# Attention ends, router and expert layer of a four-layer hybrid network rewritten, the shared expert's gate and up projections in one product

## The reference, cut to what matters

```python
t = t + _L2_attn_ref(_ln_t(t))
t = t + _L2_ffn_ref(_ln_t(t), ...)
t = t + _L3_attn_ref(_ln_t(t), ...)
t = t + _L3_ffn_ref(_ln_t(t), ...)

def _L3_ffn_ref(x, router, shared_gate, shared_up, shared_down, W_gate, W_up, W_down):
    # n = 2048 tokens, D = 128, E = 8 experts, TOP_K = 2, H = 64
    shared_out = silu(x @ shared_gate) * (x @ shared_up) @ shared_down
    probs = softmax(x @ router)
    topk_scores, topk_idx = top_k(probs, TOP_K)      # combine[n, e] = score, or 0
    gate = silu(einsum('nd,edh->enh', x, W_gate))
    up = einsum('nd,edh->enh', x, W_up)
    y = einsum('enh,ehd->end', gate * up, W_down)
    return shared_out + einsum('ne,end->nd', combine, y)
```

## Time and profile before

| | us |
|---|---|
| median of 3 runs | 683.55 |
| lowest and highest run | 678.59, 688.02 |
| profiled execution, its own time | 681.39 |
| its span, first to last instruction | 679.7 |
| PE, DVE, ACT, POOL busy | 587.7, 416.9, 339.5, 285.6 |

### The profile page before, as it was taken

One profiled execution on the slowest core, in us unless ns is written; L12 is line 12 of the kernel. 1 busy time (PEld: TensorE's weight loads), 2 busy tenths in 40 slices (PEclk: granted clock), 3 DMA queues, 4 the chain that ended last, 5 costly groups with the idle time before them and its releaser, 6 DMA issues. The chain is left out here.

```text
span 679.7 us, 10150 instructions
## 1 busy us (share of the span) xinstructions
PE 587.7 (86%) x3280; PEld 322.6 (47%) x3280; DVE 416.9 (61%) x858; ACT 339.5 (50%) x586; POOL 285.6 (42%) x656
## 2 busy tenths in 40 slices
PE   7897898894965999999999999995589998469997
PEld 6664455552755444444444444443346666443332
DVE  3553477761552877678997999797545654144343
ACT  3542356663343866766667757682314555132321
POOL 4564012334141777777868776791101223300000
PEclk9997899996785999999999999998799999569999
DMA  6800000000000000000000000000000000000000
GB/s 175 237 1 0 1 2 2 2 1 0 1 2 0 1 0 0 1 1 0 1 0 0 2 0 0 1 0 0 2 1 2 1 2 2 0 0 1 30 16 16
DMA packets 10246, 8.62 MB, mean 13 GB/s; under 512 B 4042, under 2 KB 8148, under 8 KB 10196
## 3 DMA queue, kind: packets, MB, share of 16 engines
q1 hardware_dynamic: 10196, 8.00, 4.1%
HBM read 6.94 MB, written 1.05 MB: 12 GB/s over the span
## 5 line engine op out<-in xcount | busy, mean ns | idle before, releaser
L1477 POOL TENSOR_TENSOR h_s<-g_s 128x512 f32<-128x512 f32 x128 | 163.9, 1284 | 53.3 <-ACT g_s L1411 34.2
L1411 ACT ACTIVATE g_s<-z_s,b 128x1024 f32<-128x1024 f32 x128 | 146.9, 1149 | 65.2 <-DVE z_s L1334 38.6
L1334 DVE TENSOR_TENSOR z_s<-bank,PB 128x1024 f32<-128x1024 f32 x128 | 153.5, 1219 | 31.8 <-PE bank L1269 31.4
L1269 PE MATMUL bank<-XN_C,W 128*128 128x512 f32 x256 | 130.2, 594 | 0.9 <-PEq L1069 0.9
L1276 PE MATMUL bank<-h_s,W 128*128 128x512 f32 x256 | 130.3, 593 | 0.1
L983 DVE TENSOR_REDUCE shiftpad<-bank 128x2 f32<-128x512 f32 (+1 forms) x128 | 72.3, 588 | 66.2 <-PE bank L812 35.8
L966 ACT ACTIVATE ET_all<-bank 128x512 f32<-128x512 f32 (+1 forms) x128 | 59.2, 514 | 75.9 <-PE bank L829 43.9
L1276 PEld LDWEIGHTS bank<-h_s,W 128*128 128x128 f32 x256 | 48.5, 190 | 62.0 <-issue 56.9
L1269 PEld LDWEIGHTS bank<-XN_C,W 128*128 128x128 f32 x256 | 47.0, 190 | 52.7 <-issue 44.6
L1036 POOL TENSOR_SCALAR var<-mv 128x2 f32<-128x2 f32 x16 | 3.5, 222 | 142.2 <-DVE mv L1023 142.1
L824 PE MATMUL bank<-Qp,Kp 17*128 17x256 f32 x256 | 36.4, 401 | 7.3 <-DVE Qp L996 7.2
(11 more groups left out here) (280 smaller groups left out, 1013.0 us busy)
## 6 DMA issues: line engine op xcount, KB each, us to landing
W<-in_L_ffn_W_dram SPq DMA_DIRECT2D x1, 2048.0 KB, 8.9
out_dram<-y_s SPq DMA_DIRECT2D x4, 256.0 KB, 2.2
XN_T<-in_x_dram SPq DMA_DIRECT2D x3, 256.0 KB, 5.1
XN_T<-in_x_dram SPq DMA_DIRECT2D x2, 128.0 KB, 2.2
Wgate<-in_L_ffn_W_gate_dram SPq DMA_DIRECT2D x1, 256.0 KB, 5.0
Wup<-in_L_ffn_W_up_dram SPq DMA_DIRECT2D x1, 256.0 KB, 4.3
Wdown<-in_L_ffn_W_down_dram SPq DMA_DIRECT2D x1, 256.0 KB, 4.0
wraw<-in_L_conv_W_qkv_dram SPq DMA_DIRECT2D x1, 192.0 KB
```

The lines of the kernel that those rows point to most:

```text
L1269: nc.tensor.matmul(bank[s % 4][:, :], W1[:, f // 4, f % 4 * P:(f % 4 + 1) * P], XN_C[:, g * W:(g + 1) * W], start=True, stop=True).then_in ...
L1334: nc.vector.tensor_tensor(z_s[:, s % RING, :].rearrange("p (w n) -> p w n", w=2), bank[s % 4][:, None, :].broadcast_to([P, 2, W]), PB[:, g ...
L1411: nc.scalar.activation(g_s[:, s % RING_G, :], z_s[:, s % RING, :], ACT.Gelu, bias=b1[:, f:f + 1]).then_inc(s_g, 1)
L1477: nc.gpsimd.tensor_tensor(h_s[:, s % RING, :], g_s[:, s % RING_G, 0:W], g_s[:, s % RING_G, W:2 * W], ALU.add).then_inc(s_h, 1)
```

## The change

- The attention blocks of layers 1 and 3 end when image 6 is in XN_C (step 41). Image 7's root, scaling, turning and storing move to the front of the next block (class `LastImage`): VectorE computes the root there in 12 linked steps, 11 of them linked to the next, instead of GpSimd's 16. In layer 2 this stands at VectorE's step 1, ScalarE's steps 2 and 3 and TensorE's step 3; in the expert block at the very start and at steps 0 and 1.
- In layer 2's attention the last pair's root is also computed by VectorE, not by GpSimd.
- The router block is gone. Its work is split into two halves of 8 tiles (class `ExpertWeights`, with 17 VectorE pieces numbered 0 to 16: 0 and 1 maximum and subtraction, 2 to 4 the softmax, 5 the MAX8, 6 the index search, 7 to 11 the mask, 12 to 16 the three bf16 parts). The early half runs inside layer 3's attention, its logits at steps 19, 23, 27 and 31, its VectorE pieces at steps 32 to 38, its turns and stores at steps 40 and 41. The late half runs inside the expert block's steps 2 to 9.
- The expert block is written out, 20 steps q with no loop, down products lag by two steps (before: one, inside a group), a_s and c_s have four buffers each, and two result banks take turns.
- The shared expert's gate and up weights lie side by side (Sboth), so one product gives gate on partitions 0 to 63 and up on 64 to 127. ScalarE reads rows 0 to 63 and writes its Silu to rows 64 to 127, where VectorE multiplies it with the up rows; the shared down product reads rows 64 to 127.
- The residual is no longer turned ahead and added by VectorE: four products of R with the identity per group open the result bank's accumulation. VectorE copies the bank to out_s (two buffers); the last group's copy is shared between ScalarE and VectorE.

```diff
-        Sgate = sb("Sgate", [P, EH])
-        Sup = sb("Sup", [P, EH])
-        Sdown = sb("Sdown", [EH, P])
+        Sboth = sb("Sboth", [P, 2, EH])
+        Sdown = sb("Sdown", [P, P])
...
+        class LastImage:
...
+            def dve(self, dve):
+                link, c = Chain(dve, self.s_steps), self.c
+                link(nc.vector.tensor_scalar(var[:, c:c + NT], mv[:, c:c + NT, 1], 1e-5, None, ALU.add))
+                rsqrt(nc.vector, link, c, NT)
+                nc.vector.scalar_tensor_tensor(shift[:, c:c + NT], mv[:, c:c + NT, 0], -1.0, rstd[:, c:c + NT],
+                                               ALU.mult, ALU.mult).then_inc(self.s_rs, 1)
+
+            def act_scale(self, act):
+                act.wait_ge(self.s_rs, 1)
+                for t in range(NT):
...
+                    ins = nc.scalar.activation(XN_T[:, a:a + P], R[:, a:a + P], ACT.Identity,
+                                               bias=shift[:, c:c + 1], scale=rstd[:, c:c + 1])
+                ins.then_inc(self.s_xn, 1)
+
+            def pe(self, pe, to):
+                pe.wait_ge(self.s_xn, 1)
+                for t in range(NT):
...
+                    ins = nc.tensor.transpose(to[:, t * P:(t + 1) * P], XN_T[:, a:a + P], ident[:, :])
+                ins.then_inc(self.s_xT, 1)
+
+            def act_keep(self, act, to):
+                act.wait_ge(self.s_xT, 1)
+                nc.scalar.copy(XN_C[:, self.n * N:(self.n + 1) * N], to[:, 0:N]).then_inc(self.s_done, 1)
...
-            LAST = 4 * (IMAGES - 1) + AT_XT + 1
+            LAST = 4 * (IMAGES - 2) + AT_XT + 1
...
+                        if weights is not None:
+                            if (n := image_at(s, AT_XT + 2)) is not None and n * NT < len(weights.tiles):
+                                pe.wait_ge(s_done, n + 1)
+                                weights.logits(pe, n * NT, range(n * NT, (n + 1) * NT), bank[RING_S + RING_T])
+                            if s in (LAST - 2, LAST - 1):
+                                if s == LAST - 2:
+                                    pe.wait_ge(weights.s_sh, 1)
+                                weights.turn(pe, s - LAST + 2, bank[RING_S + RING_T])
...
+                        if weights is not None:
+                            for k in WEIGHT_STEPS.get(s - BURSTS, ()):
+                                weights.dve(dve, weight_link, k, bank[RING_S + RING_T])
...
+                        if s == IMAGES - 1:
+                            pe.wait_ge(last1.s_done, 1)
...
+                    if s == 1:
+                        last1.dve(dve)
...
+                        if n == IMAGES - 1:
+                            dve.wait_ge(s_mv, n + 1)
+                            dve.wait_ge(s_xn, n - 1)
+                            link(nc.vector.tensor_scalar(var[:, 0:TILES], mv[:, 0:TILES, 1], 1e-5, None, ALU.add))
+                            rsqrt(nc.vector, link, 0, TILES)
+                            nc.vector.scalar_tensor_tensor(shift[:, 0:TILES], mv[:, 0:TILES, 0], -1.0, rstd[:, 0:TILES],
+                                                           ALU.mult, ALU.mult).then_inc(s_rs, 1)
...
-                for k in range(IMAGES // PAIR):
+                pool.wait_ge(last1.s_xn, 1)
+                for k in range(IMAGES // PAIR - 1):
...
+            def turn(self, pe, i, to):
+                if i == 0:
+                    pe.wait_ge(self.s_wp, 1)
+                else:
+                    pe.wait_ge(self.s_kept, i)
+                for j in range(TILES):
+                    ins = nc.tensor.matmul(to[0:PARTS * EXPERTS, j * P:(j + 1) * P], w_parts[:, self.tiles[0] + i * TILES + j, :, :],
+                                           identb[:, :], start=True, stop=True)
+                ins.then_inc(self.s_wT, 1)
+
+            def keep(self, act, i, to):
+                a = (self.tiles[0] + i * TILES) * P
+                act.wait_ge(self.s_wT, i + 1)
+                nc.scalar.copy(wT[:, a:a + W], to[0:PARTS * EXPERTS, :]).then_inc(self.s_kept, 1)
...
+        WEIGHT_STEPS = {0: (0, 1), 2: (2, 3, 4), 3: (5,), 4: (6, 7), 5: (8, 9, 10, 11), 6: (12, 13, 14, 15, 16)}
+        late_weights = ExpertWeights("l3_w_late", range(ALL // 2, ALL))
+        attention("l3", True, Wo3, QK3[:, 0:2, :], QK3[:, 2:4, :], None, ExpertWeights("l3_w_early", range(ALL // 2)))
...
+        D_LAG4, C_RING = 2, 4
+        LATE_STEPS = {3: (0, 1), 4: (2, 3, 4), 5: (5, 6, 7), 6: (8, 9, 10, 11), 7: (12, 13, 14, 15, 16)}
...
+                for q in range(STEPS + D_LAG4):
+                    if q < STEPS:
+                        g, b = divmod(q, BLOCKS)
+                        if q >= 2:
+                            pe.wait_ge(s_si, q - 1)
+                        if q >= 2 and (q - 2) % BLOCKS == BLOCKS - 1:
+                            pe.wait_ge(s_m, q - 1)
+                        nc.tensor.matmul(bank[q % 2][:, :], Wgate[:, 2 * b:2 * b + 2, :] if b < 4 else Sboth[:, :, :],
+                                         XN_C[:, g * W:(g + 1) * W], start=True, stop=True).then_inc(s_G, 1)
+                        if b < 4:
+                            if q >= 2:
+                                pe.wait_ge(s_m, q - 1)
+                            nc.tensor.matmul(bank[2 + q % 2][:, :], Wup[:, 2 * b:2 * b + 2, :],
+                                             XN_C[:, g * W:(g + 1) * W], start=True, stop=True).then_inc(s_Up, 1)
+                            r = g * 4 + b
+                            if r >= 2:
+                                pe.wait_ge(s_c, r - 1)
+                            if g >= 2:
+                                pe.wait_ge(late_weights.s_kept, g - 1)
+                            nc.tensor.matmul(bank[4 + r % 2][:, :], expert_rows[:, b * P:(b + 1) * P],
+                                             wT[:, g * W:(g + 1) * W], start=True, stop=True).then_inc(s_rw, 1)
+                    if (d := q - D_LAG4) >= 0:
+                        g, b = divmod(d, BLOCKS)
+                        to = bank[6 + g % 2]
+                        if b == 0:
...
+                            for t in range(TILES):
+                                a = g * W + t * P
+                                nc.tensor.matmul(to[:, t * P:(t + 1) * P], R[:, a:a + P], ident[:, :],
+                                                 start=(t == 0), stop=False, skip_group_check=True)
...
+                        nc.tensor.matmul(to[:, :], Wdown[:, b, :] if b < 4 else Sdown[EH:P, :], c_s[m, d % C_RING, :],
+                                         start=False, stop=(b == BLOCKS - 1), skip_group_check=True).then_inc(s_Dn, 1)
+                    if q == 1:
+                        last3.pe(pe, bank[B_OTHER])
+                    if q == 2:
+                        pe.wait_ge(last3.s_done, 1)
+                        late_weights.logits(pe, 0, late_weights.tiles, bank[B_OTHER])
+                    if q in (8, 9):
+                        pe.wait_ge(s_sum, 1)
+                        late_weights.turn(pe, q - 8, bank[6])
...
+                    nc.scalar.activation(a_s[m, q % C_RING, :], bank[q % 2][0:(P if q % BLOCKS < 4 else EH), :], ACT.Silu).then_inc(s_si, 1)
+                    if q == 0:
+                        last3.act_scale(act)
+                    if q == 1:
+                        last3.act_keep(act, bank[B_OTHER])
+                    if q == 3:
+                        late_weights.exp(act)
+                    if q in (8, 9):
+                        late_weights.keep(act, q - 8, bank[6])
...
+                nc.scalar.copy(out_s[0:64, g % 2, :], bank[6 + g % 2][0:64, :]).then_inc(s_sum, 1)
...
+                nc.vector.tensor_copy(out_s[64:P, g % 2, :], bank[6 + g % 2][64:P, :]).then_inc(s_sum, 1)
```

305 lines of the change are left out of this document (157 added, 148 removed).

## The result

The changed kernel runs in 659.88 us (median of 4, 656.45 to 661.15) against 684.7 for the kernel before on the same chip (4 runs, 678.59 to 688.02). The ratio is 0.964, interval 0.956 to 0.972: faster, by 25 us. The forecast was 658.0 in a range of 649 to 668. The profiled execution took 658.72, its span 656.9 (forecast 655.6 and 653.9; before 681.39 and 679.7). The span therefore fell by 22.8 and not by 25.8, and the 3.0 between them are what the experiments have to account for. The first gate product of the expert stage starts at 587.04, where the forecast said 582.3.

The account below looks back on a forecast made before the run. Engines taking turns around the router stage and TensorE's list in the expert stage were taken as bounds; -5.3 + 1.5 - 22.3 + 0.4 - 0.1 = -25.8 us, span 679.7 to 653.9, median 658, range 649 to 668.

Parts of the forecast that it names:

- Part 1: Layer 1's end and layer 2's attention: image 7's finish moved, last root on VectorE; -5.3 us, bounds -6.7 and -3.4.
- Part 2: Early router half inside layer 3's attention: eight logit products counted whole on TensorE; +1.5 us, bounds 0 and 2.
- Part 3: Joint from layer 3's attention to the expert stage, router stage gone: first gate product at 586.1 instead of 608.44, -22.3 us.
- Part 4: Expert stage: TensorE's list sets the time, 67.0 us with residual and late router work moved in; +0.4, bounds -2 and +5.
- Rival A: Expert stage: two activation table switches delay Silu 4 by 2.6 us and gate 6 stands 2 us; time 660, chance 0.14.
- B: Layer 2, joint and expert stage: displaced VectorE work is on the path everywhere, 3 us of stalls included; 664, chance 0.17.
- D: Expert stage: ring of waits makes each step last its own chain, 5.0 us, 34 us more; 692, slower, chance 0.03.
- The end: Last addition of 512 columns becomes half a copy on each of two engines, store unchanged; -0.1 us.
- C: Everything hides: pieces free at both joints, early logits within waits, -1.4 - 1.5 - 1.5; median 653, chance 0.11.

Follow-up runs that it names:

- e7: Kernel before with only image 7's finishing moved from layer 1 into layer 2's attention and the last root there on VectorE; 682.31 us, ratio 0.998.
- e10: Changed kernel with layer 1's attention again ending with image 7 and layer 2's last root back on GpSimd; 661.38 us, ratio 0.968.
- e9: Kernel before with only the shared expert's gate and up weights joined in one product; 678.05 us, ratio 0.996.
- e8: Changed kernel plus unread products (six in layer 2's attention, eight before the last q/k turns, two after image 7's projection) and early router pieces reordered; 646.93 us, ratio 0.947.
- e1: Changed kernel plus six unread f32 products of 512 columns in TensorE's idle times at the end of layer 2's attention; 652.13 us, ratio 0.953.
- e12: Changed kernel with the early half's late VectorE router pieces pulled forward, away from image 7, no added products; 661.38 us, ratio 0.966.
- e3: Changed kernel with the late router half's exponential replaced by an identity, so no activation table switch in the expert stage; 659.0 us, ratio 0.965.
- e4: Changed kernel with down products one step behind the gate products instead of two; 660.46 us, ratio 0.966.
- e2: Changed kernel plus six unread products in layer 2's attention and five before the last q/k turns of its feed-forward; 650.94 us, ratio 0.951.

## Why the prediction was right

**Part 1** (-5.3) was right for what it counted: the feed-forward starts 5.79 us earlier, against 6.7 as the bound. From the stage's first product to the second image's copy it is now 6.37 us instead of 5.12, 1.25 for image 7's root where 1.4 were let through, and the last root takes 2.3 on VectorE instead of 4.5. The part did not count TensorE's clock at the feed-forward: the feed-forward came 5.8 us earlier, the clock's return only 0.9 (220.5 instead of 221.4), and 2.1 of the 5.8 are given back at once. This is the step that failed. The forecast priced the half clock in the expert stage alone, where the kernel before showed it (0.96 in the earlier trace rows), and took the clock of 1.00 with which feed-forward and layer 3's attention started before as given, without reading those windows. In e7 and e10 the medians leave 0.5 to 2.5 us of part 1, with executions of different clock in them.

**Layer 3's attention start** cost another 2.16 us that no term held. By e9 it can fall on the old code too, so it is a price of the execution rather than of a part; it went against the forecast here, in both traces of the changed kernel (33.68 and 33.72). One of the forecast's own signs of being wrong came true by it: layer 3's attention was to be no more than 2 us longer before its last scores, and it was 88.9 instead of 85.3, 3.6 longer. The cause is not the displaced work that the sign was meant for: in e8, with the same work and the clock at 1.00, it is 86.75, 1.5 longer, the price of the eight logit products.

**Part 2** (+1.5) measured +2.50. The eight products were sized well: between two images' additions to R lie 10.19 us instead of 9.83 where two of them were put in, three times, and in e1, with the clock at 1.00, the fourth takes 7.82 instead of 7.39; together 1.5. The other 1.0 is clock once more, before image 6's addition (8.81 there in the changed kernel). TensorE's rows of the kernel before there, and behind the same idle time of 0.85 us:

```profile
575.47 0.47 PE L878 MATMUL bank<-ET_all,vall 128*17 128x160 f32 x8 [0.85 <-ACT ET_all L966]
...
576.09 0.71 PE L937 MATMUL bank<-Wo,oT 128*128 128x128 f32 x4
```

and those of the changed kernel:

```profile
575.54 0.74 PE L881 MATMUL bank<-ET_all,vall 128*17 128x160 f32 x8 [0.85 <-ACT ET_all L977]
...
576.63 1.22 PE L940 MATMUL bank<-Wo,oT 128*128 128x128 f32 x4
```

**Part 3** (-22.3) measured -22.52, for a reason that was half right. VectorE's chain from MAX8 at 579.11 to the last cast's end at 584.13 took 5.0 us with image 7's reciprocal and scaling in it, where 0.7 + 4.5 were said. But the forecast let image 7's addition set the joint, and e12 shows that taking 2.4 us off it gives 0.2. GpSimd's root of image 6, 579.27 to 583.77, is the other chain of nearly the same length, and it was not followed. That the total of this part came out within 0.2 is luck to that extent.

**Part 4** (+0.4) measured -0.03 to the last down product. The list was the right model: 66.46 busy of 66.5, no wait. A group at full clock, 621.07 to 636.33, takes 15.26 where 15.5 was said: four residual products of 128 columns are 0.99 from start to start, not 1.1, and the rest is rounding of the routed steps. In the other direction the eight late logit products took 1.71 instead of 1.5, and the start at the lower level some 2.7 (e8) instead of 2.3. Rival A was worth 0.0 (e3), B and D had no stall (e4), and the joined product gives its 0.9 a group only because the list runs on over the group's end: alone, in the old loop, it gave 0.5 (e9).

**The end** (-0.1) measured -1.37. From the last down product's start to the store's issue 1.88 instead of 2.24, and from there to the end of the span 2.6 instead of 3.5. So 0.4 is the change's. The other 1.0 is not: in e7 and e9, whose end is that of the kernel before, the store's issue to the end of the span takes 2.5 too, and in e4, whose end is the changed kernel's, 3.3. It varies between executions that end with the same code, and it went for the forecast here.

In sum: -0.5 (part 1) +2.3 +2.2 +1.0 (clock) -0.2 (joint) -0.4 (expert stage) -1.3 (end) = +3.1, the 3.0 that were missing up to rounding. That 660 came so near to 658 is in part luck: the misses have both signs, and one of those that helped, the 1.0 of the store, is chance of the execution. The lower end of the stated range, 649, is also 2 us under what the bounds of the parts add up to (651). Most of the 5.5 of clock could be had back: e8 runs in 646.93.

**The rivals.** A (660) fits the total and is false, which the total alone could not have told. C (653) failed since the early logits did cost their 1.5; the late pieces were free, as it said. B (664) failed in its place: the late pieces stall nobody.

## What to carry to other kernels

An edit that shortens the way to a stage also changes what TensorE did just before it; read the granted clock in the first 5 us of every stage behind a pause, and give it a term with both bounds, even where the profile before shows 1.00. Idle TensorE time ahead of a dense stage can be filled with products that nobody reads, but here they had to reach close to that stage's first product: six of them, with TensorE idle for 0.7 us behind the last (e1), gave 8 us of 660, and five more that ended 2.6 us early (e2) gave nothing measurable. And where two engines' chains meet at a joint, follow both to their last row before pricing the shortening of one.
